# Edge attention on one core: queries spread as two rounded parts at 256 columns, weighted sums by one product per pair of tiles

## The chip, the cores and the metric

The kernel runs on one core of a Trainium2 chip. The metric is the device time of one execution in microseconds (us). A core has a TensorE for matmuls, a VectorE, a ScalarE and a GpSimd engine, a SyncE that issues transfers, and 16 DMA engines. In the profile they are PE (matmuls), PEld (the weight loads of the matmuls), DVE, ACT, POOL and SP.

## The reference

One layer of graph attention with a residual and a layer norm: 6250 nodes of 128 features, 200000 edges sorted by their target, 8 heads of 16. The biases are drawn, not zero.

```python
q, k, v = x @ Wq + bq, x @ Wk + bk, x @ Wv + bv         # each in 8 heads of 16
scores = sum(q[dst] * k[src], axis=-1) * 0.25 + (edge_attr_64 @ We + be)
e = exp(scores - segment_max(scores, dst)[dst])
probs = e / (segment_sum(e, dst) + 1e-10)[dst]
agg = segment_sum(probs[:, :, None] * v[src], dst)       # the heads side by side
out = layernorm(x + agg @ Wo + bo)
```

## The kernel before, in words

**Tiles.** A tile is 128 edges, one per partition. A block is 28 tiles: 14 tiles of each of two halves (j = 0, 1), and each half touches a window of at most W = 64 nodes. Tiles of the two halves alternate, so that tiles 2k and 2k+1 are a pair. There are 57 blocks; the last ones are smaller. A step is four tiles, two pairs; a full block has seven steps, and there are 392 steps.

**Set-up.** k and v of all nodes are projected (line 1085) and written to a table in DRAM. POOL then gathers for each tile the 128 rows of k and v that its edges need (line 507, one indirect transfer per tile, 28 per block), into one of three buffers. The gather of a step of block b waits until the same step's place was used up by `weigh` in block b-3.

**The loop.** All engines walk the same slots v, one step each, with different parts of the work at fixed offsets. The order on every engine is written out by hand and the waits are semaphores. In slot v:

- PE runs `spread_q(v)` (line 1133), which turns the 64 queries of each half into one query row per edge by a product with a one-hot matrix; `match(v)` (lines 1110 and 1116), which makes the one-hot matrices of the next slot; `sum_step(v)` (line 1170), which adds the weighted v of four tiles, 128 value columns and 8 weight columns (136 in all), onto the nodes of a block; and at fixed slots of a block the smaller products (edge terms, transposes, query projection, projection by Wo).
- ACT copies the one-hot matrices out of PSUM (`copy_hots`, line 567), takes the exponentials (lines 598 to 600), copies weights beside the weighted v (line 608) and copies the projected queries (`copy_q`, line 587).
- DVE runs `weigh` (line 801, v times weight, twelve slots behind the queries), `multiply` (line 780, spread queries times k), `dot` (line 791, the sums of 16), and at fixed slots the running maxima of a block, `copy_halves` (line 907), `add_folded` (line 911) and the layer norm.

`sum_step(v)` comes behind `spread_q(v)` and `match(v)` on PE; DVE's `weigh(v+1)` waits for it, and `multiply(v+1)` stands behind that `weigh` on DVE. In the queries the two halves are two sets of 64 rows of the array, with a bank of PSUM each; the step uses both banks, so `spread_q(v+1)` waits for `multiply(v)`. In the sums the two halves are two sets of 64 columns of the array and write partitions 0 to 63 and 64 to 127 of one bank. Each of the four tiles has a product of its own in both. In float32 the trace shows every product as two weight loads and two matmuls.

Of the kernel before, what the change touches and what calls it, by code (L numbers as in the profile page):

```python
# [39 lines left out]
def graph_attention(nc, x_t, x_perm, src, dst, src_blk, dst_blk, dst_chk, dst_ends, dst_row, dst_seq, edge_blk, edge_t,  # L40
# [48 lines left out]
    with ctx:  # L89
# [6 lines left out]
        def sem(name):  # L96
            return ctx.enter_context(nc.semaphore(name))
# [21 lines left out]
        hots = sb("hots", [P, 2, 2, QUAD * W])  # L119
# [7 lines left out]
        q_blk = sb("q_blk", [P, QBUF, D])  # L127
# [86 lines left out]
        q_banks = ps("q_banks", [P, 2, 512])  # L214
        ps_q = [q_banks[:, i, :] for i in range(2)]
# [15 lines left out]
        def sums(b):  # L231
            return ps_a[b % 2][:, 0:WV]
# [51 lines left out]
        s_newq, s_qcopied = sem("s_newq"), sem("s_qcopied")  # L284
# [250 lines left out]
        def _(act):  # L535
# [47 lines left out]
            def copy_q(b):  # L583
                act.wait_ge(s_newq, b + 1)
                if b >= QBUF:
                    act.wait_ge(s_byedge, FIRST[b - QBUF + 1])
                act.copy(q_blk[:, b % QBUF, :], new_q).then_inc(s_qcopied, 1)
# [89 lines left out]
        def _(dve):  # L677
# [3 lines left out]
            dve.memset(eps_c[:, :], LN_EPS)  # L681
            dve.memset(carried[:, :], 0.0)
# [87 lines left out]

            def multiply(q):
                b, g = STEPS[q]
                t0, t1 = STEP[b][g]
                n = t1 - t0
                dve.wait_ge(s_byedge, q + 1)
                landed = sum(STEP[k][g][1] - STEP[k][g][0] for k in range(b % NBUF, b + 1, NBUF) if g < GS[k])
                dve.wait_ge(s_kv[b % NBUF][g], 16 * landed)
                if q >= 2:
                    dve.wait_ge(s_dot, q - 1)
                dve.tensor_tensor(prod[:, q % 2, 0:n * D].rearrange("p (k j d) -> p j k d", j=2, d=D),  # L780
                                  q_banks[:, :, 0:n // 2 * D].rearrange("p j (k d) -> p j k d", d=D),
                                  kv_buf[:, b % NBUF, t0:t1, 0:D].rearrange("p (k j) d -> p j k d", j=2),
                                  ALU.mult).then_inc(s_product, 1)
# [119 lines left out]
            def copy_halves(b):  # L903
                dve.wait_ge(s_carrysum, b + 1)
                if b >= 2:
                    dve.wait_ge(s_left, b - 1)
                dve.tensor_copy(sums_sb[:, b % 2, :], sums(b)).then_inc(s_halves, 1)
# [33 lines left out]
            with dve.If(general == 0):  # L941
                for v in SLOTS:
# [23 lines left out]
                    if at_node(v, 8) is not None:  # L966
                        normalise(at_node(v, 8))
            with dve.Else():
# [98 lines left out]
        def _(pe):  # L1067
# [53 lines left out]
            def spread_q(v):  # L1121
# [3 lines left out]
                pe.wait_ge(s_qcopied, b + 1)  # L1125
                pe.wait_ge(s_copied, HOTS_TO[v - 1])
                if q >= 1:
                    pe.wait_ge(s_product, q)

                for u in range(t1 - t0):  # L1130
                    j, k = u % 2, u // 2
                    own = slice(j * W, (j + 1) * W)
                    one = pe.matmul(ps_q[j][:, k * D:(k + 1) * D], hots[own, (v - 1) % 2, 0, k * P:(k + 1) * P],  # L1133
                                    q_blk[own, b % QBUF, :], start=True, stop=True)
# [22 lines left out]
            def sum_step(v):  # L1157
# [10 lines left out]
                for u in range(t1 - t0):  # L1168
                    own = slice(u % 2 * W, (u % 2 + 1) * W)
                    one = pe.matmul(sums(b)[own, :], hots[:, (v - 1) % 2, 1, u * W:(u + 1) * W], wv[:, q % 2, u, :],  # L1170
                                    start=(t0 + u < 2), stop=False)
                one.then_inc(s_summed, 1)

            def sum_carry(b):
                if b >= 1:
                    pe.wait_ge(s_carried, b)
                pe.matmul(sums(b), ident[0:1, :], carried[:, :], start=False, stop=True).then_inc(s_carrysum, 1)
# [190 lines left out]
```

## Time and profile before

| | |
|---|---|
| median of 3 runs | 2608.14 us (2605.48 to 2614.73) |
| the profiled execution, its own time | 2609.25 us |
| its span, first to last instruction | 2607.4 us |
| mean granted clock of TensorE | 0.647 of full speed |
| busy: PE, PEld, DVE, ACT, POOL | 54%, 36%, 51%, 16%, 58% |
| gathers issued by POOL | 1564, mean 959 ns |
| DMA | 290.29 MB, 111 GB/s |

A busy share is that of instructions as they are recorded. The recorded end of a matmul is modelled; when an engine that waits for PE in fact went on is read from the start of that engine's next instruction. A granted clock of 1.0 is 2.4 GHz, one of 0.5 is 1.2 GHz. "Remote" and "another core or an unknown queue" are the profile's names for a wait whose end it could ascribe to no recorded instruction's end; there is only one core here.

### The profile page before, as it was taken

To read this page: it belongs to the slowest core of one execution; us is meant where nothing else is said; L and a number is where in the kernel's file an instruction comes from. 1 tells how busy PE (TensorE), PEld (TensorE's weight loads), DVE (VectorE), ACT (ScalarE), POOL (GpSimd) and SP (SyncE) were. 2 spreads that over 40 slices of the span, in tenths; PEclk is the share of its full clock that TensorE was granted. 3 is DMA by queue.
4 is the path that set the end of the run, shared out by engine and by line. 5 is a ranking of instruction groups with operands and counts; after the bars stand their busy time and mean duration, and the time that the engine had idled before them with its cause. 6 is when DMAs were issued, how large, how long until landed. Compare 5 with 4: busy or idle time off the path is not lost.

```text
span 2607.4 us, 30805 instructions
## 1 busy us (share of the span) xinstructions
PE 1395.8 (54%) x9699; PEld 933.4 (36%) x9699; DVE 1341.0 (51%) x3136; ACT 420.9 (16%) x1427; POOL 1521.0 (58%) x1578
## 2 busy tenths in 40 slices
PE   4145555455645464555555555546464545555557
PEld 3033333333433343333334333334343333333334
DVE  4045455554555554545555545555454545555556
ACT  0011111111111111111111111111111111111112
POOL 6735656566566566565556565656566665656540
PEclk7555666666667666666666666666566666566666
DMA  7423333333333333333333333333333333333320
GB/s 271 140 82 97 117 103 103 118 102 124 100 118 106 120 103 121 101 109 113 101 119 105 118 108 117 104 116 106 120 104 123 100 124 95 108 117 106 119 88 7
DMA packets 115466, 290.29 MB, mean 111 GB/s; under 512 B 45765, under 2 KB 53712, under 8 KB 108264
## 3 DMA queue, kind: packets, MB, share of 16 engines
q0 software_dynamic: 75072, 205.10, 26.3%
q1 hardware_dynamic: 37484, 76.52, 8.7%
q10 hardware_dynamic: 2748, 6.69, 0.7%
q8 instruction: 80, 1.31, 0.2%
q14 instruction: 82, 0.67, 0.1%
HBM read 276.52 MB, written 11.67 MB: 111 GB/s over the span
## 4 chain that ended last, share of the span: by engine, by line
another core or an unknown queue 37%; PE 34%; DVE 18%; issue 8%; ACT 2%; DMA 1%; SPq 0%; DVEq 0%; ACTq 0%
PE q_banks L1133 12%; PE ps_a L1170 7%; DVE prod L780 4%; DVE score L791 3%; PE ps_e L1145 2%; PE ps_t L1110 2%; PE ps_s L1191 2%; DVE wv L801 1%; PE ps_t L1116 1%; DVE run_fwd L843 1%; PE ps_a L1212 1%; PE ps_s L1197 1%; PE ps_a L1222 1%; DVE cand L837 1%
## 5 line engine op out<-in xcount | busy, mean ns | idle before, releaser
L507 POOL DMA_INDIRECT kv_buf<-kv_table,src_i x1564 | 1499.1, 959 | 1013.8 <-DVE wv L801 569.0
L1133 PE MATMUL q_banks<-q_blk,hots 64*128 64x128 f32 x3128 | 416.4, 405 | 537.3 <-issue 263.0
L1133 PEld LDWEIGHTS q_banks<-q_blk,hots 64*128 64x128 f32 x3128 | 319.4, 277 | 655.1 <-issue 635.0
L567 ACT ACTIVATE hots<-ps_t 128x512 f32<-128x512 f32 x377 | 225.1, 597 | 1972.9 <-PE ps_t L1116 960.8
L780 DVE TENSOR_TENSOR prod<-q_banks,kv_buf 128x512 f32<-128x512 f32 (+1 forms) x392 | 269.0, 686 | 410.8 <-remote 265.5
L801 DVE TENSOR_TENSOR wv<-kv_buf,ps_w 128x512 f32<-128x512 f32 (+1 forms) x392 | 265.6, 678 | 362.8 <-remote 334.8
L1170 PE MATMUL ps_a<-wv,hots 128*64 128x136 f32 x3128 | 376.5, 379 | 5.6 <-ACT wv L608 4.8
L1212 PE MATMUL ps_a<-sums_sb,carry_from 128*1 128x136 f32 x112 | 34.3, 409 | 542.2 <-DVE sums_sb L911 542.2
L791 DVE TENSOR_REDUCE score<-prod 128x32 f32<-128x512 f32 (+1 forms) x392 | 267.1, 681 | 7.9 <-issue 0.2
L1170 PEld LDWEIGHTS ps_a<-wv,hots 128*64 128x64 f32 x3128 | 239.9, 183 | 68.3 <-issue 51.2
L1212 PEld LDWEIGHTS ps_a<-sums_sb,carry_from 128*1 128x1 f32 x112 | 4.8, 81 | 564.1 <-DVE sums_sb L911 564.1
L911 DVE TENSOR_TENSOR sums_sb<-ps_a,sums_sb 1x136 f32<-1x136 f32 x57 | 16.9, 297 | 328.5 <-remote 327.0
L1116 PE MATMUL ps_t<-node_code,codes 128*128 128x128 bf16 x782 | 141.6, 276 | 1.6 <-ACT hots L571 1.6
L1110 PE MATMUL ps_t<-codes,node_code 128*128 128x256 bf16 (+1 forms) x392 | 139.7, 356 | 0.5 <-DMA codes<-code_table 0.5
L861 DVE TENSOR_TENSOR_SCAN ps_s<-seq_far,seq_left,ps_s 8x512 f32<-8x512 f32 x57 | 72.7, 1276 | 95.2 <-issue 71.4
L1116 PEld LDWEIGHTS ps_t<-node_code,codes 128*128 128x128 bf16 x782 | 94.6, 122 | 23.0 <-ACT hots L571 2.7
L608 ACT COPY wv<-weight 128x32 f32<-128x32 f32 (+1 forms) x392 | 96.6, 246 | 0.0
L1110 PEld LDWEIGHTS ps_t<-codes,node_code 128*128 128x128 bf16 x392 | 42.1, 107 | 108.8 <-issue 97.4
L1145 PE MATMUL ps_e<-edge_f,w_e 128*32 128x512 f32 (+1 forms) x456 | 68.6, 678 | 0.0
L867 DVE TENSOR_TENSOR_SCAN seq_b<-seq_far,ps_s 8x512 f32<-8x512 f32 x57 | 68.3, 1198 | 0.0
L1154 PE MATMUL ps_e<-ident,terms_t 128*128 128x128 f32 x224 | 60.2, 421 | 0.0
L1207 PE MATMUL ps_s<-w_qkv,xt_blk 128*128 128x128 f32 x114 | 44.2, 441 | 28.7 <-issue 28.6
(141 smaller groups left out, 1337.5 us busy)
## 6 DMA issues: line engine op xcount, KB each, us to landing
edge_f<-in_edge_blk SPq DMA_DIRECT2D x55, 1024.0 KB
kv_buf<-kv_table,src_i POOLq DMA_INDIRECT x1564
kv_table<-kv_buf ACTq DMA_DIRECT2D x12, 512.0 KB, 4.4
xt_blk<-in_x_t SPq DMA_DIRECT2D x114, 32.0 KB
out<-y_out SPq DMA_DIRECT2D x114, 32.0 KB
kv_buf<-in_x_perm SPq DMA_DIRECT2D x5, 512.0 KB, 7.8
codes<-code_table SPq DMA_DIRECT2D x108, 10.5 KB
code_table<-kv_buf SPq DMA_DIRECT2D x1, 1344.0 KB
```

The source lines that it names most:

```text
L507: pool.indirect_dma_start(kv_buf[:, b % NBUF, t, :], None, kv_table, bass.IndirectOffsetOnAxis(ap=src_i[:, column:column + 1], axis=0)).th ...
L567: one = act.activation(hots[:, v % 2, :, :].rearrange("p k n -> p (k n)"), ps_t[:, :], ACT.Relu, bias=1.0)
L608: act.copy(wv[:, q % 2, 0:t1 - t0, D:WV], by_head(weight[:, b % 2, :], TILES[b])[:, :, t0:t1].rearrange("p h t -> p t h")).then_inc(s_besi ...
L780: dve.tensor_tensor(prod[:, q % 2, 0:n * D].rearrange("p (k j d) -> p j k d", j=2, d=D), q_banks[:, :, 0:n // 2 * D].rearrange("p j (k d) ...
L791: dve.tensor_reduce(score[:, b % 2, :, t0:t1].rearrange("p h t -> p t h"), prod[:, q % 2, 0:(t1 - t0) * D].rearrange("p (t h d) -> p t h d ...
L801: dve.tensor_tensor(wv[:, q % 2, 0:t1 - t0, 0:D].rearrange("p t (h d) -> p t h d", d=HD), kv_buf[:, b % NBUF, t0:t1, D:KV].rearrange("p t ...
L861: dve.tensor_tensor_scan(turned_ends, far[:, 0:SEQ], turned_ends, left, ALU.add, ALU.max).then_inc(s_seqf, 1)
L1110: one = pe.matmul(ps_t[:, 0:(t1 - t0) * W], node_code[:, :], codes[:, b % CBUF, t0 * W:t1 * W], start=True, stop=True)
L1116: one = pe.matmul(ps_t[:, QUAD * W + k * P:QUAD * W + (k + 1) * P], codes[:, b % CBUF, t0 * W + k * P:t0 * W + (k + 1) * P], node_code[:, ...
L1133: one = pe.matmul(ps_q[j][:, k * D:(k + 1) * D], hots[own, (v - 1) % 2, 0, k * P:(k + 1) * P], q_blk[own, b % QBUF, :], start=True, stop=True)
L1145: one = pe.matmul(ps_e[at:at + P // EGROUPS, 0:n * P].rearrange("k (s p) -> k s p", p=P), w_e2[:, :], edge_f[:, b % 2, :].rearrange("k (s ...
L1170: one = pe.matmul(sums(b)[own, :], hots[:, (v - 1) % 2, 1, u * W:(u + 1) * W], wv[:, q % 2, u, :], start=(t0 + u < 2), stop=False)
```

## The change

The queries are copied out of PSUM three times instead of once: in full (`q_full`), and each half rounded to the type F32R into its own columns of `q_part`, where the other half's columns stay zero. DVE then subtracts the rounded part from the full one (`low_q`) and stores the rest as a second part, rounded too. The spread of a pair is then two products, accumulated, of all 128 rows by 256 columns: rounded part, then rest. A step has four such products. Each step writes one bank, and the two banks alternate, so that `spread_q` waits for the product of the step before the last one. The one-hot matrices are stored as F32R; the sums read the same bytes as float32. The weighted sums of a pair are one float32 product with 128 columns of weights (both halves' one-hots) by 272 columns (both tiles' values and weights); of its result the two blocks on the diagonal are read, by two copies in `copy_halves`, one of 64 partitions each.

```diff
-        hots = sb("hots", [P, 2, 2, QUAD * W])
+        hots = sb("hots", [P, 2, 2, QUAD * W], F32R)
...
-        q_blk = sb("q_blk", [P, QBUF, D])
+        q_full = sb("q_full", [P, D])
+        q_part = sb("q_part", [P, QBUF, 2, 2 * D], F32R)
...
-        q_banks = ps("q_banks", [P, 2, 512])
-        ps_q = [q_banks[:, i, :] for i in range(2)]
+        ps_q = [ps(f"ps_q{i}", [P, 512]) for i in range(2)]
...
-            return ps_a[b % 2][:, 0:WV]
+            return ps_a[b % 2][:, 0:2 * WV]
+
+        def half_sums(b, j):
+            return ps_a[b % 2][j * W:(j + 1) * W, j * WV:(j + 1) * WV]
...
             def copy_q(b):
                 act.wait_ge(s_newq, b + 1)
+                if b >= 1:
+                    act.wait_ge(s_qlow, b)
                 if b >= QBUF:
                     act.wait_ge(s_byedge, FIRST[b - QBUF + 1])
-                act.copy(q_blk[:, b % QBUF, :], new_q).then_inc(s_qcopied, 1)
+                act.copy(q_part[0:W, b % QBUF, 0, 0:D], new_q[0:W, :])
+                act.copy(q_part[W:P, b % QBUF, 0, D:2 * D], new_q[W:P, :])
+                act.copy(q_full[:, :], new_q).then_inc(s_qcopied, 1)
...
+            dve.memset(q_part[:, :, :, :].rearrange("p b k d -> p (b k d)").bitcast(F32), 0.0)
...
+            def low_q(b):
+                dve.wait_ge(s_qcopied, b + 1)
+                dve.tensor_tensor(q_part[0:W, b % QBUF, 1, 0:D], q_full[0:W, :], q_part[0:W, b % QBUF, 0, 0:D], ALU.subtract)
+                dve.tensor_tensor(q_part[W:P, b % QBUF, 1, D:2 * D], q_full[W:P, :], q_part[W:P, b % QBUF, 0, D:2 * D],
+                                  ALU.subtract).then_inc(s_qlow, 1)
...
-                dve.tensor_tensor(prod[:, q % 2, 0:n * D].rearrange("p (k j d) -> p j k d", j=2, d=D),
-                                  q_banks[:, :, 0:n // 2 * D].rearrange("p j (k d) -> p j k d", d=D),
-                                  kv_buf[:, b % NBUF, t0:t1, 0:D].rearrange("p (k j) d -> p j k d", j=2),
-                                  ALU.mult).then_inc(s_product, 1)
+                dve.tensor_tensor(prod[:, q % 2, 0:n * D].rearrange("p (t d) -> p t d", d=D),
+                                  ps_q[q % 2][:, 0:n * D].rearrange("p (t d) -> p t d", d=D),
+                                  kv_buf[:, b % NBUF, t0:t1, 0:D], ALU.mult).then_inc(s_product, 1)
...
-                dve.tensor_copy(sums_sb[:, b % 2, :], sums(b)).then_inc(s_halves, 1)
+                for j in range(2):
+                    one = dve.tensor_copy(sums_sb[j * W:(j + 1) * W, b % 2, :], half_sums(b, j))
+                one.then_inc(s_halves, 1)
...
             with dve.If(general == 0):
+                for b in range(min(QBUF, NB)):
+                    low_q(b)
                 for v in SLOTS:
...
+                    if chain(v, 6) is not None and chain(v, 6) + QBUF < NB:
+                        low_q(chain(v, 6) + QBUF)
...
-                pe.wait_ge(s_qcopied, b + 1)
+                pe.wait_ge(s_qlow, b + 1)
                 pe.wait_ge(s_copied, HOTS_TO[v - 1])
-                if q >= 1:
-                    pe.wait_ge(s_product, q)
-
-                for u in range(t1 - t0):
-                    j, k = u % 2, u // 2
-                    own = slice(j * W, (j + 1) * W)
-                    one = pe.matmul(ps_q[j][:, k * D:(k + 1) * D], hots[own, (v - 1) % 2, 0, k * P:(k + 1) * P],
-                                    q_blk[own, b % QBUF, :], start=True, stop=True)
+                if q >= 2:
+                    pe.wait_ge(s_product, q - 1)
+                for k in range((t1 - t0) // 2):
+                    for part in range(2):
+                        one = pe.matmul(ps_q[q % 2][:, k * 2 * D:(k + 1) * 2 * D], hots[:, (v - 1) % 2, 0, k * P:(k + 1) * P],
+                                        q_part[:, b % QBUF, part, :], start=(part == 0), stop=(part == 1))
...
-                for u in range(t1 - t0):
-                    own = slice(u % 2 * W, (u % 2 + 1) * W)
-                    one = pe.matmul(sums(b)[own, :], hots[:, (v - 1) % 2, 1, u * W:(u + 1) * W], wv[:, q % 2, u, :],
-                                    start=(t0 + u < 2), stop=False)
+                for k in range((t1 - t0) // 2):
+                    one = pe.matmul(sums(b), hots.bitcast(F32)[:, (v - 1) % 2, 1, k * P:(k + 1) * P],
+                                    wv[:, q % 2, 2 * k:2 * k + 2, :].rearrange("p j w -> p (j w)"),
+                                    start=(t0 + k == 0), stop=False)
                 one.then_inc(s_summed, 1)
...
-                pe.matmul(sums(b), ident[0:1, :], carried[:, :], start=False, stop=True).then_inc(s_carrysum, 1)
+                pe.matmul(sums(b)[:, 0:WV], ident[0:1, :], carried[:, :], start=False, stop=True).then_inc(s_carrysum, 1)
```

## Rows read from the trace of the kernel before

**Rows 1.** The page's busy times of the engines, their share and instructions:
```profile
PE 1395.8 (54%) x9699; PEld 933.4 (36%) x9699; DVE 1341.0 (51%) x3136; ACT 420.9 (16%) x1427; POOL 1521.0 (58%) x1578
```

**Rows 2.** The page's chain that ended last, by engine, and its lines:
```profile
another core or an unknown queue 37%; PE 34%; DVE 18%; issue 8%; ACT 2%; DMA 1%; SPq 0%; DVEq 0%; ACTq 0%
```

**Rows 3.** Groups of instructions by line (busy us, mean ns | idle before, releasers):
```profile
L507 POOL DMA_INDIRECT kv_buf<-kv_table,src_i x1564 | 1499.1, 959 | 1013.8 <-DVE wv L801 569.0 <-issue 432.5 <-DMA kv_table<-kv_buf 12.3
L1133 PE MATMUL q_banks<-q_blk,hots 64*128 64x128 f32 x3128 | 416.4, 405 | 537.3 <-issue 263.0 <-DVE prod L780 127.7 <-ACT hots L567 98.7
L1170 PE MATMUL ps_a<-wv,hots 128*64 128x136 f32 x3128 | 376.5, 379 | 5.6 <-ACT wv L608 4.8 <-ACT hots L571 0.7
```

**Rows 4.** The waits: engine, line, releaser; us in total, times, longest us:
```profile
DVE wv L801 <- remote: 334.8, 62, 7.0
DVE sums_sb L911 <- remote: 327.0, 46, 8.9
DVE prod L780 <- remote: 265.5, 68, 29.8
```

**Rows 5.** Line 911, once per block, between 1000 and 1500 us:
```profile
L911 DVE TENSOR_TENSOR sums_sb<-ps_a,sums_sb x12: 297/297/298, 1000.1 to 1488.8; 1x136 f32<-1x136 f32 x12
```

**Rows 6.** Timeline, 1634 to 1655 us (start, length, engine, line; idle before and releaser):
```profile
1634.39 1.23 PE L1133 MATMUL q_banks<-q_blk,hots 64*128 64x128 f32 x8
...
1635.55 0.40 PE L1110 MATMUL ps_t<-codes,node_code 128*128 128x256 bf16 x1
...
1635.74 0.42 PE L1116 MATMUL ps_t<-node_code,codes 128*128 128x128 bf16 x2
...
1636.09 1.17 PE L1170 MATMUL ps_a<-wv,hots 128*64 128x136 f32 x8
...
1638.44 0.69 DVE L780 TENSOR_TENSOR prod<-q_banks,kv_buf 128x512 f32<-128x512 f32 x1 [1.42 <-remote]
...
1639.14 0.60 ACT L567 ACTIVATE hots<-ps_t 128x512 f32<-128x512 f32 x1 [4.07 <-remote]
...
1647.05 0.69 DVE L801 TENSOR_TENSOR wv<-kv_buf,ps_w 128x512 f32<-128x512 f32 x1 [5.59 <-remote]
...
1649.84 0.69 DVE L780 TENSOR_TENSOR prod<-q_banks,kv_buf 128x512 f32<-128x512 f32 x1 [2.10 <-remote]
...
1652.69 0.60 ACT L567 ACTIVATE hots<-ps_t 128x512 f32<-128x512 f32 x1 [12.01 <-remote]
...
1654.24 0.69 DVE L801 TENSOR_TENSOR wv<-kv_buf,ps_w 128x512 f32<-128x512 f32 x1 [2.99 <-remote]
...
1655.19 0.95 POOL L507 DMA_INDIRECT kv_buf<-kv_table,src_i  x1 [2.49 <-DVE wv L801]
```

**Rows 7.** Stretches: us, busy us and instructions of each engine, granted clock, DMA:
```profile
1639.14:1652.69 13.55, 5.53 (x29) 3.96 (x29) 4.29 (x14) 1.54 (x8) 9.34 (x10) 0.55 0.33 97
1634.39:1637.26 2.87, 2.87 (x21) 1.96 (x19) 2.53 (x6) 0.69 (x2) 2.26 (x3) 0.52 0.33 101
```

**Rows 8.** Timeline of DVE behind the last gather, line 801 one block apart:
```profile
2540.03 0.69 DVE L801 TENSOR_TENSOR wv<-kv_buf,ps_w 128x512 f32<-128x512 f32 x1
...
2560.92 0.69 DVE L801 TENSOR_TENSOR wv<-kv_buf,ps_w 128x512 f32<-128x512 f32 x1
```

**Rows 9.** Timeline of PE in the set-up, four records (two products) each:
```profile
25.67 1.03 PE L1085 MATMUL ps_t<-w_qkv,kv_buf 128*128 128x256 f32 x4
26.53 1.03 PE L1085 MATMUL ps_w<-w_qkv,kv_buf 128*128 128x256 f32 x4
```

**Rows 10.** Stretches as in Rows 7, at granted clock 1.0:
```profile
1323.15:1324.80 1.65, 1.65 (x21) 1.16 (x19) 1.32 (x3) 0.57 (x2) 1.30 (x2) 1.00 0.24 79
25.67:27.39 1.72, 1.72 (x9) 1.52 (x8) 1.38 (x3) 0.00 (x0) 0.00 (x0) 1.00 0.80 324
```

**Rows 11.** Groups by line, for the small operations added:
```profile
L923 DVE TENSOR_TENSOR agg_n<-sums_sb,rec 128x128 f32<-128x128 f32 x57 | 16.8, 294 | 2.0
...
L587 ACT COPY q_blk<-ps_s 128x128 f32<-128x128 f32 x57 | 14.8, 260 | 33.0 <-PE ps_s L1207 24.2 <-issue 8.8
```

More of the change, by code:

```diff
@@ L283, in graph_attention @@
         s_weighted, s_beside, s_summed = sem("s_weighted"), sem("s_beside"), sem("s_summed")
-        s_newq, s_qcopied = sem("s_newq"), sem("s_qcopied")
+        s_newq, s_qcopied, s_qlow = sem("s_newq"), sem("s_qcopied"), sem("s_qlow")
         s_changes, s_runends = sem("s_changes"), sem("s_runends")
```

## The prediction

> **What bounds the kernel now.** The page comes first: no engine is busy for more than 58% [rows 1], and 37% of the chain that ended last is time for which the profile has no cause [rows 2]. So the loop waits, and the question is on what. Line 911 runs once per block, and its first and last start give the block's period: (1488.8 - 1000.1)/11 = 44.4 us [rows 5]. POOL's row comes next. A gather takes 959 ns and 432.5/1401 = 0.31 us of issue goes ahead of it, so the 28 gathers of a block need 28 x 1.27 = 35.5 us; the rest of POOL's idle time is a wait for `weigh`, which frees the buffers [rows 3]. A block is thus **35.5 us in which POOL gathers and 8.9 us in which it waits**.
>
> What keeps `weigh` back is seen in the timeline [rows 6]. The products of one step (1133, 1110, 1116, 1170) are recorded from 1634.39 to 1637.26, 2.9 us. What waits for them goes on much later: `multiply` at 1638.44, the copy of the one-hots at 1639.14, `weigh` at 1647.05, ten microseconds behind the last sum's recorded end. The next `multiply` follows at 1649.84 and the next copy at 1652.69. POOL ran out of permitted gathers at 1655.19 - 2.49 = 1652.70; from then on things go fast, and `weigh` for a sum recorded long before starts at 1654.24. The waits say the same in total: 334.8 + 327.0 + 265.5 = 927 us before lines 801, 911 and 780 end as "remote" [rows 4]. Behind the last gather there is no such delay, and a whole block of slots passes in 2560.92 - 2540.03 = 20.9 us [rows 8], though the late blocks are a little smaller. My reading: **while POOL gathers, PE's completions reach the others late, at a limited rate; when it stops, the backlog clears at once.** POOL is then both the floor (35.5 us) and the cause of the rest.
>
> What sets that rate? Between the copies at 1639.14 and 1652.69 the completions of one sum (8 weight loads, 8 matmuls), one spread (8 and 8), one set of four transposes (4 and 4) and one match (3 and 3) came through: 46 instructions of PE. In the same 13.55 us DVE and ACT did 14 and 8 [rows 7]. That is 68 instructions, 0.20 us each. The stretch with one sum and nearly all 22 of the others took 7.9 us (1639.14 to 1647.05), that with one spread and hardly another 2.8 us. So the rate goes with the number of instructions, those of DVE and ACT among them, and not with the work in them. I take this as the likeliest law; it is an inference from one stretch.
>
> **The change part by part.**
>
> *Instructions removed.* A step's spread falls from 8 + 8 instructions on PE to 4 + 4, if an F32R product is one load and one matmul. Its sums fall from 8 + 8 to 4 + 4: two float32 products in place of four. That is 16 per step, 112 per block. A block has 2 x 9699/57 = 340 on PE, 3136/57 = 55 on DVE and 1427/57 = 25 on ACT [rows 1], 420 in all. The change adds two on ACT and three on DVE. It becomes 420 - 112 + 5 = 313, three quarters.
>
> *What that is worth.* Let f be the share of a block that gets through while POOL gathers; the rest runs undisturbed. By the 0.20 us, f = 35.5/(420 x 0.20) = 0.42, and the other 0.58 took the 8.9 us. With 313 instructions f = 35.5/62.6 = 0.57, the rest takes 8.9 x 0.43/0.58 = 6.6 us, and a block gains 2.3 us. By the block without gathers [rows 8], f = 1 - 8.9/20.9 = 0.57, an instruction costs 35.5/(0.57 x 420) = 0.148 us, f becomes 0.77 and the rest 4.8 us: a gain of 4.1 us. I use both ends: 2.3 to 4.1 us by 55 blocks is 126 to 226 us, **middle 176 us**.
>
> *PE's own work.* A float32 product of 256 columns on the full array streams for (26.53 - 25.67)/2 = 0.43 us at 2.4 GHz [rows 9, 10], so one of 272 columns for 0.46 us, and 0.91 us at 1.2 GHz. Two of them are 1.83 us against 1.17 us for the four now, whose halves run side by side [rows 6]: +0.66 us per step at 1.2 GHz, half of that at 2.4 GHz. The F32R product is not in the trace. The nearest rows are a bf16 product of 256 columns, after which the next starts 0.19 us later at 1.2 GHz (1635.55 to 1635.74 [rows 6]), and the float32 product, 0.86 us at 1.2 GHz. So four cost between 0.8 and 3.4 us, against 1.23 us now. I take the low end, 0.85 us, because the kernel splits the query into two rounded parts, which is only of use if each is a single pass. Net +0.3 us per step at 1.2 GHz, +2.1 us per block. It counts only in the part of a block that runs undisturbed (0.23 to 0.43) and there as far as PE is last: 0.5 to 0.9 us per block, **+40 us**. With the high end of the F32R price it is +2.9 us per step and +260 us.
>
> The Trainium skill says on this (FP8 and Floating Point Precision, "TensorE Precision Notes") that true float32 takes four passes through the array and that reduced-precision float32 reads the four bytes truncated. By that page an F32R product would cost a quarter of a float32 one, as at my low end; no run here shows it yet.
>
> *The wait between spread and multiply.* PE waits 127.7 us in all at line 1133 for `multiply` [rows 3], 2.2 us per block. With two banks that wait looks one step further back and mostly goes. The sums and `weigh` still tie PE to DVE one slot later, so I count a third, **-40 us**, between 0 and -128.
>
> *Small operations.* `low_q` is two subtractions of 64 x 128; the nearest row is 128 x 128 at 294 ns [rows 11], so 0.2 to 0.3 each, and `copy_halves` gets one more: 0.8 us of DVE per block. ACT's two further copies are 260 ns each [rows 11], 0.5 us per block. DVE is the engine that follows PE closely when nothing disturbs (0.23 to 0.43 of a block), so 0.2 to 0.35 us per block, **+15 us**; if that cover went, +45 us. `low_q` waits for ACT's copy, and that for PE's query projection, with `weigh` of the next slot queued behind it on DVE. That `weigh` waits for a sum which PE issues after the projection, so the new wait ends no later than the old one: 0. ACT's copy waits for the previous `low_q`, a block earlier: 0. PE waits for `low_q` three blocks ahead of use: 0. Behind ACT's longer `copy_q` stand the weight copy of that slot and next slot's one-hots; they wait for a later completion of PE anyway. Should ACT take longer to write one-hots as F32R than now, there is ample idle time (busy 16%), but each stands in the path from match to spread; 0 to 0.1 us per step, I take 0. No transfer is added or moved. The memset and the first three `low_q` lie under the first gathers: 0, at most 3 us.
>
> *Sum.* -176 + 40 - 40 + 15 = -161 us against the profiled execution's 2609.25 us (span 2607.4 and 1.9 around it): 2448 us. The median of the runs is 1 us lower, which doesn't matter. I take 2450 us.
>
> **The rivals.**
>
> 1. *Only part of the fall* (0.20). The F32R product keeps two loads and two matmuls, or two passes, or the instructions of the sums weigh more than those of the spread. If only the sums' 8 instructions per step go, half of the 176 us stays: about 2530 us.
>
> 2. *Slower* (0.17). The delayed completions have to do with the gathers alone and not with the number of instructions. For it: every release in the timeline falls near the end of a run of gathers [rows 6]. Against it: the different length of stretches with few and many instructions. Then f stays 0.42 to 0.57, PE's +2.1 us per block counts for about half, +1.05 us, and DVE's 0.8 for as much, +0.4 us; by 55 blocks +80 us, 2690 us. It decides once PE's step without disturbance exceeds DVE's, which three lines of 0.68 us make about 2.1 us: at 1.2 GHz PE is at 2.9 us already. One page speaks on this side. The Trainium skill (TensorE: Matmul & The Clock Gate, "Measured speedup vs the span model") has products on separate columns of the array running at once, which the change gives up in the sums; the trace agrees, since eight records of 1170 take 1.17 us at a mean of 379 ns each. By that rule alone the sums cost 0.66 us more per step.
>
> 3. *Much faster* (0.10). With a quarter of the instructions gone the backlog hardly forms, and POOL is the floor: 35.5 us and 1.5 us of hand-over per block, 2609 - 55 x 7.4 = 2200 us.
>
> 4. *No change* (0.05): gains and PE's work cancel, 2608 us.
>
> My forecast has 0.48. Its own range, from the ends of its terms, is 2380 to 2520 us. To hold eight in ten it must reach to rival 1 and well toward rivals 2 and 3: **2310 to 2690 us**. The chances of faster (forecast, rivals 1 and 3): 0.78; same within 0.3%, about what can be told from no change: 0.05; slower: 0.17.
>
> **What would show it.** Right: PE and PEld near 6600 instructions each; the period of line 911 near 41 us; the "remote" waits of 801, 911 and 780 down by a third or more from 927 us; POOL's wait for `weigh` well under 569 us; line 1170 with 1568 records whose starts lie 0.45 us apart at 1.2 GHz. Wrong: as many records as before at 1133 (rival 1); remote waits as long as before with fewer instructions (rival 2); or the F32R products recorded at 0.8 us each, which would carry the time above 2700 us.

## The result, and the profile after

The kernel after takes **2704.93 us** (median of 4 runs, 2694.68 to 2713.66), the kernel before beside it 2611.43 us (2605.48 to 2619.45): **ratio 1.0363, interval [1.0329, 1.0396]**. It is slower; I had predicted 2450 us, which is faster. The profiled execution takes 2713.66 us, with a span of 2711.8 us.

Busy times, granted clock and chain from the page of after:

```profile
PE 1440.7 (53%) x6571; PEld 1010.9 (37%) x6571; DVE 1378.0 (51%) x3308; ACT 456.0 (17%) x1541; POOL 1507.3 (56%) x1578
...
PEclk7567766676676767676666667676776767677677
...
another core or an unknown queue 26%; issue 26%; PE 23%; DVE 23%; ACT 1%; ACTq 0%; DVEq 0%; DMA 0%
```

Groups by line of after (columns as in [rows 3]), then line 927, once per block (`add_folded`, as in [rows 5]), and the waits (as in [rows 4]):

```profile
L511 POOL DMA_INDIRECT kv_buf<-kv_table,src_i x1564 | 1485.4, 950 | 1133.2 <-DVE wv L815 685.5 <-issue 436.7 <-DMA kv_table<-kv_buf 11.1
L1187 PE MATMUL ps_a<-wv,hots 128*128 128x272 f32 x1564 | 643.0, 551 | 55.5 <-issue 47.2 <-ACT wv L616 5.6 <-DVE wv L815 2.5
L1151 PE MATMUL ps_q<-q_part,hots 128*128 128x256 f32 x1564 | 399.4, 393 | 922.8 <-issue 920.3 <-ACT hots L571 2.0 <-ACT hots L575 0.5
```

```profile
L927 DVE TENSOR_TENSOR sums_sb<-ps_a,sums_sb x24: 297/297/298, 413.4 to 1482.7; 1x136 f32<-1x136 f32 x24
```

```profile
ACT hots L571 <- remote: 1249.9, 130, 22.4
...
DVE prod L795 <- remote: 539.7, 56, 35.0
...
DVE wv L815 <- remote: 262.5, 39, 12.4
DVE ps_s L875 <- remote: 256.4, 47, 7.8
```

ACT's wait at the same place in the kernel before, the copy of the one-hots:

```profile
ACT hots L567 <- remote: 920.8, 136, 15.5
```

PE has a third fewer instructions, as the change says. But the block now takes (1482.7 - 413.4)/23 = 46.5 us in place of 44.4, and POOL's wait for `weigh` (line 815 here) has grown from 569.0 to 685.5 us. That is +116.5 us against +104.4 us of span: **the whole loss stands in that one wait**. POOL's own gathers and issue take 1485.4 + 436.7 = 1922 us, against 1932 us in [rows 3]. The remote waits have moved (911 has left the list, `multiply`, line 795, took over) and not shrunk: the three longest of DVE's sum to 539.7 + 262.5 + 256.4 = 1059 us, against the 927 us of [rows 4], and ACT's grew from 920.8 to 1249.9 us.

The timeline of after, the same place in a slot as [rows 6]:

```profile
1411.37 1.19 PE L1151 MATMUL ps_q<-q_part,hots 128*128 128x256 f32 x4 [2.55 <-issue]
...
1412.36 0.44 PE L1130 MATMUL ps_t<-codes,node_code 128*128 128x256 bf16 x1
...
1412.81 2.13 PE L1187 MATMUL ps_a<-wv,hots 128*128 128x272 f32 x4
...
1417.10 0.69 DVE L815 TENSOR_TENSOR wv<-kv_buf,ps_w 128x512 f32<-128x512 f32 x1 [6.89 <-remote]
...
1423.87 0.95 POOL L511 DMA_INDIRECT kv_buf<-kv_table,src_i  x1 [0.30 <-issue]
1428.26 0.69 DVE L795 TENSOR_TENSOR prod<-ps_q,kv_buf 128x512 f32<-128x512 f32 x1 [10.47 <-remote]
1428.31 0.60 ACT L571 ACTIVATE hots<-ps_t 128x512 fp32r<-128x512 f32 x1 [16.48 <-remote]
...
1429.01 1.20 PE L1151 MATMUL ps_q<-q_part,hots 128*128 128x256 f32 x4 [14.07 <-issue]
```

PE's products for the next steps of DVE and ACT are recorded by 1414.94. But for one `weigh` at 1417.10, DVE and ACT go on only at 1428.3, after the last gather that POOL was allowed (its end is at 1424.8). All three then run at full pace. Fewer instructions were sent and they came through no sooner. A step of PE also got longer: from the first spread to the end of the sums 1414.94 - 1411.37 = 3.57 us, against 2.87 us in [rows 7], at a granted clock of 0.50 and 0.52.

### The profile page after: what moved, and what is told of

It is laid out like the page before. It is cut to its first block, busy times and chain, and to the rows that moved or that the text cites. A ratio compares the mean times of both kernels' runs of the same rounds, so it can differ in the third digit from the quotient of the medians.

```text
span 2711.8 us, 24837 instructions
## 1 busy us (share of the span) xinstructions
PE 1440.7 (53%) x6571; PEld 1010.9 (37%) x6571; DVE 1378.0 (51%) x3308; ACT 456.0 (17%) x1541; POOL 1507.3 (56%) x1578
## 4 chain that ended last, share of the span: by engine, by line
another core or an unknown queue 26%; issue 26%; PE 23%; DVE 23%; ACT 1%; ACTq 0%; DVEq 0%; DMA 0%
PE ps_a L1187 9%; PE ps_q L1151 6%; DVE prod L795 5%; DVE wv L815 3%; DVE score L805 3%; DVE ps_s L875 2%; DVE seq_b L881 2%; PE ps_t L1130 1%; PE ps_t L1136 1%; DVE run_fwd L857 1%; DVE run_max L860 1%; PE ps_s L1215 1%; PE ps_a L1230 1%; PE ps_e L1163 1%
## 5 line engine op out<-in xcount | busy, mean ns | idle before, releaser
L511 POOL DMA_INDIRECT kv_buf<-kv_table,src_i x1564 | 1485.4, 950 | 1133.2 <-DVE wv L815 685.5
L1151 PE MATMUL ps_q<-q_part,hots 128*128 128x256 f32 x1564 | 399.4, 393 | 922.8 <-issue 920.3
L1151 PEld LDWEIGHTS ps_q<-q_part,hots 128*128 128x128 f32 x1564 | 307.6, 266 | 1008.2 <-issue 993.9
L1187 PE MATMUL ps_a<-wv,hots 128*128 128x272 f32 x1564 | 643.0, 551 | 55.5 <-issue 47.2
L571 ACT ACTIVATE hots<-ps_t 128x512 fp32r<-128x512 f32 x377 | 225.0, 597 | 1980.4 <-remote 1249.9
L795 DVE TENSOR_TENSOR prod<-ps_q,kv_buf 128x512 f32<-128x512 f32 (+1 forms) x392 | 266.9, 681 | 571.1 <-remote 539.7
L815 DVE TENSOR_TENSOR wv<-kv_buf,ps_w 128x512 f32<-128x512 f32 (+1 forms) x392 | 265.7, 678 | 378.8 <-remote 262.5
L1187 PEld LDWEIGHTS ps_a<-wv,hots 128*128 128x128 f32 x1564 | 376.3, 266 | 125.7 <-issue 59.8
L875 DVE TENSOR_TENSOR_SCAN ps_s<-seq_far,seq_left,ps_s 8x512 f32<-8x512 f32 x57 | 72.7, 1276 | 277.0 <-remote 256.4
L1240 PE MATMUL ps_a<-bias_row,ones 1*128 1x128 f32 x114 | 28.6, 332 | 86.5 <-ACT agg_t L624 86.5
L1240 PEld LDWEIGHTS ps_a<-bias_row,ones 1*128 1x128 f32 x114 | 17.3, 190 | 110.1 <-ACT agg_t L624 109.8
L1209 PE MATMUL ps_s<-ident,ends 128*8 128x128 f32 x228 | 54.5, 387 | 1.4 <-issue 0.8
```

Of the source, the lines that this page charges most:

```text
L511: pool.indirect_dma_start(kv_buf[:, b % NBUF, t, :], None, kv_table, bass.IndirectOffsetOnAxis(ap=src_i[:, column:column + 1], axis=0)).th ...
L571: one = act.activation(hots[:, v % 2, :, :].rearrange("p k n -> p (k n)"), ps_t[:, :], ACT.Relu, bias=1.0)
L795: dve.tensor_tensor(prod[:, q % 2, 0:n * D].rearrange("p (t d) -> p t d", d=D), ps_q[q % 2][:, 0:n * D].rearrange("p (t d) -> p t d", d=D) ...
L815: dve.tensor_tensor(wv[:, q % 2, 0:t1 - t0, 0:D].rearrange("p t (h d) -> p t h d", d=HD), kv_buf[:, b % NBUF, t0:t1, D:KV].rearrange("p t ...
L875: dve.tensor_tensor_scan(turned_ends, far[:, 0:SEQ], turned_ends, left, ALU.add, ALU.max).then_inc(s_seqf, 1)
L1151: one = pe.matmul(ps_q[q % 2][:, k * 2 * D:(k + 1) * 2 * D], hots[:, (v - 1) % 2, 0, k * P:(k + 1) * P], q_part[:, b % QBUF, part, :], sta ...
```

## The experiments

Eighteen runs were made, in six sessions on five chips (the second and the last on the same one). Letters in the expectations name theories. In experiment 1 A and B mean what each expectation says. From experiment 2 on, A says that the delay and the loss belong to the kernel, and C that the late completions are a condition of a chip, and that the gathers alone set the time where it is absent.

**1. Where is the loss? Gathers away, and each part alone (first session).** The gathers of blocks 3 to 56 are left out, so the products read old rows of k and v, and the output is not the reference's.

```diff
-                for b in range(1, NB):
+                for b in range(1, NBUF):
                     gather(b)
```

> The kernel before, but POOL gathers only for the first three blocks, and the products of all later blocks read what those left in the three buffers; every other instruction stays. Theory A (PE's completions are held back only while POOL gathers): a block takes 19 to 23 us as behind the last gather, so some 1250 to 1450 us in all, and hardly any wait ends as remote. Theory B (the remote waits have nothing to do with gathers): well over 2000 us with the remote waits kept.

> The changed kernel with the same cut: gathers only for the first three blocks. Theory A (the change lost because PE's own step became longer, which counts only where no gather disturbs): slower than the other kernel without gathers, by about a fifth, 3 to 4 us per block, 150 to 220 us in all. Theory B (PE's longer work is hidden and the change lost in the part with gathers): within 50 us of it.

> The changed kernel with the sums put back: four products of 64 columns of weights by 136 columns per step, and one copy. Theory A (the sums' doubled work is the loss): 2580 to 2620 us, level with before or slightly faster. Theory B (the spread, its two banks and low_q cost the time): near 2700 us. The law of the prediction (0.15 to 0.20 us per instruction saved): 2500 to 2550 us.

> The kernel before with only the sums changed: one product of 128 columns by 272 columns per pair, and the two copies. Theory A: 2680 to 2730 us, all of the loss. Theory B: near 2610 us. The law of the prediction: 2520 to 2560 us, since 8 instructions of PE per step are gone.

The kernels with one part are the change's own hunks: spread alone keeps the four sum products of 64 columns of weights, sums alone keeps `q_blk` and the old spread.

Measured: the kernel before, unchanged, takes **2051.75 us** on the chip of these runs, not 2611. Spread alone: 2052.86, ratio 1.0002 [0.9993, 1.0012]. Sums alone: 2047.73, 0.9981 [0.9971, 0.9990]. Without the gathers before takes 1640.9 and after 1617.07 us (one run each). The two expectations with gathers were for a kernel of 2611 us and say nothing here. Without them neither A (1250 to 1450 us) nor B (well over 2000 us) had the time of before. For after, A's 150 to 220 us slower is refuted and B's within 50 us holds: it is 24 us faster.

**2. Is that the chip? Both kernels again (second session).**

> The kernel before, unchanged, on the chip of these runs, for its profile there. Theory C (the completions that reach the others late are a state of the chip of the first measurement, and without them the gathers set the time): 28 gathers of 1.27 us per block make 35.5 us, about 2050 us in all, POOL never waits for weigh, and the remote waits are gone. Theory A (the delay belongs to the kernel): 2600 us with some 900 us of remote waits.

> The changed kernel, unchanged, on the same chip as before_again. Theory C: 2045 to 2060 us if before is at 2050 us, since both are bound by the same 1564 gathers; slower by 3 to 4% only if before is at 2600 us. Theory A: slower by 3 to 4% wherever it runs.

Measured: before 2052.85 us (profiled execution), its runs 2051.54 in the median; after 2051.67, **ratio 1.000 [0.9991, 1.001]**. Page (busy times, chain) and POOL's waits of the kernel before there:

```profile
PE 1386.5 (68%) x9699; PEld 897.2 (44%) x9699; DVE 1330.4 (65%) x3136; ACT 426.2 (21%) x1427; POOL 1511.1 (74%) x1578
...
POOL 71%; issue 24%; PE 3%; DVE 1%; DMA 1%; ACT 0%; ACTq 0%; POOLq 0%; DVEq 0%
```

```profile
POOL kv_buf L507 <- issue: 474.0, 1556, 0.3
...
POOL kv_buf L507 <- DVE wv L801: 2.1, 7, 0.3
```

The busy times are those of [rows 1] within 1.3%, those of the weight loads (PEld) 4% shorter, so the engines are about equally fast. What is gone is the wait: 2.1 us for `weigh` in place of 569.0, no remote wait, and a chain that is POOL and its issue for 95%. The time is the gather floor. C holds: **the same kernel takes 2611 us on one chip and 2052 us on another, and only on the first kind does this change move the time by more than 0.2%.** I call chips of the first kind late, the others prompt. Each session was on one chip, and no late chip was measured in two of them, so whether it is the chip itself or something of the session that makes completions late is not shown. A count goes with it that has nothing to do with PE: of SyncE's 1628 instructions 304 last longer than 0.6 us in the first profile of before and 163 in that of after; here it is 5 and 3.

The traces also record when each semaphore was updated, and that shows whose completions come late. I leave out the last 3 us, where all semaphores are updated once more, and take each update against the last recorded end before it. In the first profile of before, 699 of PE's 1633 updates come over 1 us behind, and 682 of these belong to products that end while POOL gathers. Those of a step's sums come 1.4 us behind in the median, one in twenty over 11 us. On the prompt chip none of PE's 1785 is over 0.1 us behind, and those of DVE and ACT come within 0.02 us on both. One more thing differs: the late trace holds 12464 updates in all and the prompt one 36475, though the kernel is the same. So it can't be excluded that the recording itself has a part in the delay; no run tests that.

**3. What the change does where nothing else is in the way (third session, prompt chip).** Again without the gathers of blocks 3 to 56.

```diff
-                if q >= 2:
-                    pe.wait_ge(s_product, q - 1)
+                if q >= 1:
+                    pe.wait_ge(s_product, q)
```

This is the edit of the third kernel, the kernel after with the old wait; the first two are one part each, without gathers.

> Both parts' kernels of this call gather only for the first three blocks and reuse those rows later, so the loop is seen without the gather floor; the same form of the kernel before took 1640.9 us (chain: PE 59%, DVE 27%) and of the kernel after 1617.1 us (DVE 59%, PE 22%). Here the spread is the new one and the sums are the old ones. Theory S (the gain of 24 us is the spread's: its looser wait and its four short products take PE off the path): 1610 to 1622 us, the chain mostly DVE. Theory U (the gain is the sums': fuller use of the array raises the granted clock, and with it every product of PE): 1636 to 1650 us, the clock near the 0.73 of before, the chain still mostly PE.

> No gathers behind the third block; the new sums beside the old spread, so with the old wait of the spread for the product just before it. Theory U: 1615 to 1625 us with a granted clock of 0.80 or more. Theory S: 1640 us or more, since PE's own work per step has grown and the wait stands; if the clock stayed at 0.73 the sums alone would add up to 0.66 us to each of some 390 steps as far as PE is last, up to 1750 us.

> No gathers behind the third block; the kernel after in all but one wait: the spread waits again for the product just before it, as in the kernel before. If the looser wait carries the gain of 24 us, this takes 1635 us or more; if it carries nothing, within 3 us of 1617 us. My prediction had counted the looser wait as 40 us of gain (0 to 128).

> The kernel before with the new spread and its looser wait, the sums as before; gathers as before. On a chip where the kernel before takes about 2052 us both theories expect 2052 us, ratio 1.000, since 1564 gathers of 1.27 us fill the time. On a chip where the kernel before takes about 2610 us it tells which part loses the 3.6% there: ratio near 1.036 if the F32R spread with its extra ACT and DVE steps does it, 1.00 or less if the sums do it.

Measured: spread alone **1560.3 us**, sums alone **1560.84**, both with the old wait 1616.5, and (from the first session) both 1617.07, none 1640.9. With gathers, spread alone 2052.28, ratio 1.0005 [0.9995, 1.0015]. These runs without gathers are one execution each. The looser wait shows no effect in them. Either part alone gains 80 us, and the two together 24: that was expected by neither S nor U. The chain and two groups of DVE, `multiply` and the scan behind the `ends` transposes, say why. Before:

```profile
PE 59%; DVE 27%; issue 8%; POOL 4%; ACT 1%; DMA 1%; DVEq 0%; ACTq 0%; POOLq 0%
...
L780 DVE TENSOR_TENSOR prod<-q_banks,kv_buf 128x512 f32<-128x512 f32 (+1 forms) x392 | 268.7, 686 | 150.1 <-PE q_banks L1133 123.4
...
L861 DVE TENSOR_TENSOR_SCAN ps_s<-seq_far,seq_left,ps_s 8x512 f32<-8x512 f32 x57 | 72.7, 1276 | 89.2 <-PE ps_s L1191 89.2
```

Spread alone:

```profile
DVE 61%; PE 21%; issue 11%; POOL 5%; DVEq 1%; DMA 1%; ACT 0%; POOLq 0%; ACTq 0%
...
L792 DVE TENSOR_TENSOR prod<-ps_q,kv_buf 128x512 f32<-128x512 f32 (+1 forms) x392 | 267.1, 681 | 52.3 <-PE ps_q L1146 32.2
...
L872 DVE TENSOR_TENSOR_SCAN ps_s<-seq_far,seq_left,ps_s 8x512 f32<-8x512 f32 x57 | 72.7, 1276 | 78.8 <-PE ps_s L1204 78.8
```

Sums alone:

```profile
DVE 45%; PE 39%; issue 10%; POOL 5%; DVEq 1%; DMA 0%; ACT 0%; POOLq 0%; ACTq 0%
...
L783 DVE TENSOR_TENSOR prod<-q_banks,kv_buf 128x512 f32<-128x512 f32 (+1 forms) x392 | 266.9, 681 | 54.6 <-PE q_banks L1138 28.7 <-issue 20.9 <-DMA kv_buf<-kv_table,src_i 4.5
...
L864 DVE TENSOR_TENSOR_SCAN ps_s<-seq_far,seq_left,ps_s 8x512 f32<-8x512 f32 x57 | 72.7, 1275 | 90.0 <-PE ps_s L1196 90.0
```

Both parts:

```profile
DVE 59%; PE 22%; issue 12%; POOL 4%; DVEq 1%; DMA 1%; ACT 0%; POOLq 0%; ACTq 0%
...
L795 DVE TENSOR_TENSOR prod<-ps_q,kv_buf 128x512 f32<-128x512 f32 (+1 forms) x392 | 267.4, 682 | 47.5 <-PE ps_q L1151 25.5
...
L875 DVE TENSOR_TENSOR_SCAN ps_s<-seq_far,seq_left,ps_s 8x512 f32<-8x512 f32 x57 | 72.7, 1275 | 113.4 <-PE ps_s L1209 113.4
```

Either part takes most of PE off DVE's path: `multiply` waits 32 or 29 us for it instead of 123, and DVE is the larger part of the chain, though with the sums alone PE still has 39% of it. From there a second part has little left to gain and its price is seen. By the pages DVE is busy 1363.0 us with both against 1341.7 with the spread alone (16.7 of it the second copy of the sums), and that scan waits 34.6 us longer, most likely because PE does the transposes behind the longer sums. That is 21.3 + 34.6 = 56 of the 57 us between the two. Counted from the sums alone (DVE busy 1332.8 us), it is 30.2 + 23.4 = 54 of 56 us.

**4. On a late chip, which part loses? (fourth session).**

> The changed kernel once more. If the 3.6% belong to a condition in which completions come late (theory C), this run shows them only together with a kernel before of about 2610 us and some 160 to 300 SyncE instructions longer than 0.6 us; with a kernel before of about 2051 us it takes 2051 us, ratio 1.000. If they belong to the changed kernel (theory A), the ratio is about 1.036 whatever the kernel before takes.

> The kernel before with only the new sums. With a kernel before of 2051 us: ratio 0.998 to 1.000, as in the first run of it. With a kernel before of about 2610 us it tells the parts apart: about 1.036 if the long full-width sums hold back the completions, 1.00 or less if the F32R spread with its extra steps on ACT and DVE does.

This chip is late: before takes 2641.55 us. After: 2690.68, **ratio 1.0182 [1.0145, 1.0219]**. Sums alone: 2721.09, **ratio 1.0308 [1.0273, 1.0344]**. So the loss is there again, if smaller, and the sums alone lose more than both parts. Theory A, 1.036 wherever the kernel runs, is refuted by the 1.000 of experiment 2 and the 1.018 here.

**5. The spread alone, instructions against work, and the gathers on a late chip (fifth session).** `sums_split` is the kernel after with each product of 272 columns in two of 136, except the first pair of a block:

```diff
-                    one = pe.matmul(sums(b), hot, wv[:, q % 2, 2 * k:2 * k + 2, :].rearrange("p j w -> p (j w)"),
-                                    start=(t0 + k == 0), stop=False)
+                        for j in range(2):
+                            one = pe.matmul(sums(b)[:, j * WV:(j + 1) * WV], hot, wv[:, q % 2, 2 * k + j, :],
+                                            start=False, stop=False)
```

> The kernel before with only the new spread. Where the kernel before takes 2640 us, the new sums alone gave 1.031 and both parts 1.018; if the two parts simply add, this gives 1.018/1.031 = 0.988. Theory I (the late completions go by the number of instructions, my prediction): 8 of 16 instructions per step are gone here, as in the sums alone, so the spread should move the time as much as the sums did, +3%. Theory W (PE's working time decides: every microsecond that PE works longer is one in which nobody can follow): PE's busy time falls, ratio 0.98 to 0.99. Where the kernel before takes 2051 us: 1.000 again.

> The kernel after, but each full-width product of 272 columns in two of 136 (the first pair of a block excepted): the same columns through the array, and some 3000 instructions more on PE and on its weight loads, 9585 in place of 6571, about as many as in the kernel before. Theory I: on a chip with late completions this loses against the kernel after, by 8 instructions per step of 0.15 to 0.20 us in about half of a block, some 50 to 200 us. Theory W: no loss against the kernel after beyond 10 us (PE streams as long). Where the kernel before takes 2051 us both give 2051.

> The kernel before without the gathers of blocks 3 to 56. It took 1640.9 us on a chip where the full kernel takes 2052. If the late completions need the gathers (theory C), it takes 1641 us within 10 on a chip where the full kernel takes 2640 too, without remote waits. If that chip delays completions by itself, it takes clearly more, 1750 us or above.

> The kernel after without the gathers of blocks 3 to 56, 1617.1 us on a chip with 2052 for the full kernel. Theory C: 1617 us within 10 on any chip.

This chip too is late: before 2609.63 us. Spread alone: 2617.58, **ratio 1.0018 [0.9989, 1.0047]**. Split sums: 2631.65, **ratio 1.0068 [1.0040, 1.0096]**. The spread alone met none of its three expectations (0.988, +3%, 0.98 to 0.99). The split form has 8021 instructions on PE, not 9585: a product is two records of PE and two of its loads, so 1450 more on each.

POOL's wait for `weigh` (us in total, times, longest) in the four profiles, in the order after, sums alone, spread alone, split sums; a fence each:

```profile
POOL kv_buf L511 <- DVE wv L815: 679.2, 160, 30.6
```

```profile
POOL kv_buf L510 <- DVE wv L804: 693.6, 152, 37.6
```

```profile
POOL kv_buf L508 <- DVE wv L812: 583.4, 131, 30.6
```

```profile
POOL kv_buf L511 <- DVE wv L815: 582.9, 108, 30.5
```

Against the 569.0 of [rows 3] these are +110, +125, +14 and +14 us, and the spans (2719.7, 2730.0, 2620.8, 2630.1 against 2607.4) are +112, +123, +13 and +23. There is no profile of the kernel before on these two chips, so this compares across chips. On the chip of experiment 4 before takes 2641.55 us, and the profiled executions of after and of the sums alone are the longest of their runs (2721.54 and 2731.81 us); in medians the two lose 49 and 80 us there. The comparison shows where the time goes: in POOL's wait for `weigh`, and so in how far the loop gets while POOL gathers. Only in the split form 9 of the 23 us lie elsewhere. Counted from the records between 400 and 1500 us, with 0.30 us of issue for each run of gathers, a step (one start of `dot`) that falls in such a run takes 6.04 us of gathering before, 6.66 and 6.66 after, 6.84 with the sums alone, 5.93 with the spread alone and 5.90 with the split sums. Other ways to bound a run move each by up to 0.2 us, so the last two are not told apart, nor with certainty from the kernel before.

The kernels without gathers take 1704.16 and 1669.33 us here, 63 and 52 more than on the prompt chip; C had said within 10. The windows show where that is. Windows of the kernel before without gathers (us, then busy us and count of PE, PEld, DVE, ACT, POOL, the clock, DMA), on the prompt chip and on the late one:

```profile
100.00:150.00 50.00, 34.99 (x219) 23.46 (x219) 30.32 (x67) 9.45 (x31) 33.28 (x36) 0.57 0.40 119
...
400.00:1000.00 600.00, 497.92 (x3762) 333.31 (x3761) 505.69 (x1188) 165.91 (x550) 0.00 (x0) 0.75 0.14 46
```

```profile
100.00:150.00 50.00, 3.42 (x17) 1.26 (x17) 2.76 (x4) 0.38 (x1) 32.68 (x35) 0.50 0.32 94
...
400.00:1000.00 600.00, 497.96 (x3762) 333.49 (x3758) 504.88 (x1188) 165.85 (x550) 0.00 (x0) 0.75 0.14 46
```

Behind the last gather (it ends at 143 to 144 us) the two chips do the same work in the same time. In the 50 us with gathers PE is busy 35.0 us on the prompt chip and **3.4 us** on the late one. The first `weigh` starts 75.1 us later on the late chip, the 51st 62.9 us and the last of the 392 still 63.2 us: all of the difference is made around those 84 gathers. The waits of that stretch on the late chip name it:

```profile
ACT hots L571 <- remote: 83.5, 3, 45.8
```

So the late completions need the gathers: that half of C is shown, and the 10 us bound was wrong only since three blocks of gathers were left in.

**6. After and split sums on one chip (sixth session).**

> The kernel after, on the same chip as the split sums. Where the kernel before takes 2051 us: 1.000. Where it takes 2600 to 2650 us: 1.015 to 1.036, from the two earlier measurements.

> Theory G (where completions come late, what costs is the length of one product on the array, since a longer one holds back more of what others wait for, and not the number of products): 0.7% above the kernel before as in its first measurement, and 1 to 3% below the kernel after on the same chip. Theory V (chips or calls differ, the split does nothing): the same as the kernel after within 0.3%. Theory I (my prediction, number of instructions): above the kernel after. Where the kernel before takes 2051 us, nothing is told apart.

The chip was prompt (before 2051.81 us): 2050.09, ratio 0.999 [0.9981, 0.9999], and 2050.08, ratio 0.9991 [0.9982, 1.0]. Nothing is told apart; whether splitting wins back the loss on one late chip stays open.

## Why the prediction was wrong

**What bounds the kernel: right for a late chip.** 28 x 1.27 = 35.5 us of gathers per block was the floor: on prompt chips a block takes 35.2 us and the kernel 2052 us. What I took for a property of the kernel, the late completions, is a condition of the chip or the session it ran in. The reading that it is PE's completions, and those under the gathers, is confirmed by the semaphore updates of experiment 2. The profile of before did not give that away; it was one execution on one chip.

**The instructions: right.** PE and PEld have 6571 each; I had said near 6600. **The F32R product** is one load and one matmul: 1564 records, four of them recorded in 1.19 us at 1.2 GHz. The page of the Trainium skill that I had weighed (FP8 and Floating Point Precision, "TensorE Precision Notes") gives true float32 four passes through the array; a quarter of that price for an F32R product was my inference. The trace agrees roughly: 1.19 us for 4 x 256 columns is 1.2 ns a column, 2.13 us for the 2 x 272 float32 columns of the sums 3.9 ns, a factor of 3.4.

**The step that failed: "What that is worth",** the 176 us gained by 0.148 to 0.20 us per instruction. The 0.20 us came from one stretch of 13.55 us, and the 0.148 us from the 20.9 us of a late, smaller block [rows 8]; a full block without gathers takes 27.3 us. By the law a step under the gathers should have become a quarter shorter; it became 0.6 us longer (6.04 to 6.66). Three runs contradict it. The sums alone remove 8 of the 16 instructions per step and lose 3.1%. The spread alone removes as many and changes nothing. The split sums put 2900 back and measure 1.007, no worse than the 1.018 and 1.036 of the kernel after on the other late chips. I had not tested it on a second stretch.

**PE's own work: mis-sized.** I had +0.3 us per step at 1.2 GHz. The recorded step grew by 3.57 - 2.87 = 0.70 us: the sums by 2.13 - 1.17 = 0.96 instead of 0.66, and from the start of the spread to the next product 0.99 instead of 1.16 us, a saving of 0.17 instead of 0.38. One sum there is off: the +260 us for the high F32R price is 2.9 us per step at the low end of the undisturbed share (0.23); at the middle that gives +40 us it would be some 370. **The product wait** (-40): the kernel with the old wait differs by 0.6 us without the gathers, so it shows no effect there; with the gathers of a late chip it was not tested. **Small operations** (+15): DVE is busy 37 us longer (1378.0 against 1341.0), near what was counted (0.8 us per block is 46); it is hidden wherever the gathers or the completions set the time.

**Rival 2 is the side that came true,** and its 2690 us is near: the delay goes with the gathers and not with the number of instructions. Its price has another make-up, so that nearness is partly luck. It charged PE's work in the part of a block without gathers only. Measured, a block waits 44.4 - 35.2 = 9.2 us before and 46.5 - 35.1 = 11.4 us after. Without gathers a block takes 27.3 us before and 26.8 after. If the waits pass at that pace, 66% of a block got through under the gathers before and 58% after. By this estimate the loss arises under the gathers.

**What in the sums causes it is open.** PE's working time alone does not fit: a step's sums are recorded with 2.13 us in the split form as well, and that form has steps of 5.90 us under the gathers; in all PE is busy 1492.2 us in it, more than in the kernel after (1440.7). The granted clock does not fit either (0.685 in the split form, 0.684 and 0.676 in after), nor does the use of the full width of the array, which both have. The length of one product (272 columns against 136) fits all five late measurements (1.036, 1.018 and 1.031 with it, 1.002 and 1.007 without). But the split form and the unsplit one were never measured on one late chip, and before itself differs by 1.2% between late chips. I count it as the best candidate, not as shown. Nor is it shown what delays PE's completions on a late chip, and why the ratio of after was 1.036 on one and 1.018 on another.

**No variant beats the kernel before** by anything that counts: the best is the sums alone on a prompt chip, 0.998, and they lose 3.1% on a late one.

## What to carry to other kernels

Measure before and after on more than one chip before explaining a wait that has no releaser: here 21% of the time was the chip's or the session's, and whether the change cost anything hung on it. Where one engine's floor (1564 gathers of 1.27 us) is within reach of the time, take its work away once: it showed in one run that the arithmetic beside it needs 1641 of 2052 us. And a law fitted to one stretch of a trace has to be tested on a second before a sum is built on it; two improvements that free the same engine need not add, while their prices do (here 80 and 80 us made 24).

## What the runs showed of the hardware that was not expected

- The kernel before, medians by session: 2050.7 to 2051.8 us on the three prompt chips (experiments 1, 2, 3 and 6), and 2641.6 and 2609.6 us on those of experiments 4 and 5, as 2611 us in the first measurement; nothing between. On late chips PE's completions reach the other engines late while POOL issues gathers (updates of the sums 1.4 us late in the median, 24 ns on a prompt chip; PE busy 3.4 of 50 us), and hardly otherwise (498.0 of 600 us on both kinds).
- Short instructions of SyncE are affected too: 304, 163 and 172, 310, 384 and 336 of 1628 last over 0.6 us on late chips (before, after twice, sums alone, spread alone, split sums), 2 to 5 on prompt ones; without the gathers it is 31 and 39 on a late chip.
- The full-width sums go with a higher granted clock where the gathers set the time. On prompt chips it is 0.67 to 0.69 before, 0.693 with the spread alone, 0.774 with the sums alone and 0.779 with both. Without gathers either part raises it: 0.731 before, 0.822 spread alone, 0.898 sums alone, 0.86 both. The higher clock does not pay for the full-width sums on its own: with gathers PE is busy 1386.5 us before, 1445.8 with the sums alone, 1230.3 with the spread alone and 1293.8 with both. So the fall with both parts is the spread's.
